# Expert loop with the hidden units on partitions, biases outside the products, and sums made in the output tensor

## The reference, cut to what matters

```python
gate = xt @ Wg + bg
scores, idx = jax.lax.top_k(gate, 2)
h = gelu(einsum('td,edh->eth', xt, W1) + b1[:, None, :])       # 8 experts, 768 -> 384
y = einsum('eth,ehd->etd', h, W2) + b2[:, None, :]             # 384 -> 768
out = einsum('te,etd->td', comb, y)                            # comb: the scores, 0 elsewhere
x = x + out
```

## Time and profile before

| | us |
|---|---|
| median of 3 runs | 1122.59 |
| the profiled execution | 1124.31 |
| its span, first to last instruction | 1122.6 |
| first matmul of the expert loop | 901 |
| last scaled tile | 1102.1 |
| copy to the output issued | 1108.2 |

### The profile page before, as it was taken

The page is one execution under the profiler, slowest core; times in us unless marked ns, Lnnn a source line. Parts: engine busy times, 40 slices in busy tenths (PEclk is TensorE's granted clock), DMA queues, the critical chain, the costliest instruction groups (busy, mean ns, idle before and its releaser), DMA issues.

```text
span 1122.6 us, 17243 instructions
## 1 busy us (share of the span) xinstructions
PE 977.9 (87%) x6460; PEld 708.2 (63%) x6460; DVE 760.7 (68%) x1704; ACT 332.5 (30%) x402; POOL 117.2 (10%) x123
## 2 busy tenths in 40 slices
PE   3799999999789979989988988969887399999991
PEld 2677776765454445545678988858865366666660
DVE  6576788877875686986587898599979823332221
ACT  3561122112004332522333333215335232222220
POOL 3000000000001000000000000000631123333321
PEclk9789999999989999999989999969898599999996
DMA  7350121134341826637687100006056545556546
GB/s 237 105 167 29 57 86 58 57 128 176 107 178 35 297 87 233 185 101 251 225 318 298 47 1 1 1 0 254 5 186 227 209 103 102 109 112 113 110 59 166
DMA packets 58521, 146.44 MB, mean 130 GB/s; under 512 B 11386, under 2 KB 30732, under 8 KB 55434
## 3 DMA queue, kind: packets, MB, share of 16 engines
q1 hardware_dynamic: 49514, 116.25, 29.6%
q0 software_dynamic: 6048, 21.24, 10.0%
q10 hardware_dynamic: 2880, 7.87, 1.8%
HBM read 95.94 MB, written 53.23 MB: 133 GB/s over the span
## 4 chain that ended last, share of the span: by engine, by line
PE 66%; DVE 21%; issue 4%; DMA 4%; ACT 3%; SPq 1%; DVEq 0%; POOLq 0%; ACTq 0%
PE PS L1733 39%; PE PS L1982 12%; DVE arena L1449 3%; PE PS L1809 3%; DVE arena L1455 3%; DVE arena L1493 3%; PE PS L2133 2%; PE PS L1789 1%; PE PS L1820 1%; PE PS L1824 1%; DVE arena L1465 1%; DMA arena<-in_L_gnn_W_dram 1%; DVE arena L1355 1%; DVE arena L1205 1%; DMA arena<-as_d 1%
## 5 line engine op out<-in xcount | busy, mean ns | idle before, releaser
L1733 PE MATMUL PS<-arena 128*128 128x384 f16 (+7 forms) x3396 | 573.0, 322 | 4.6 <-DVE arena L1719 1.9
L1733 PEld LDWEIGHTS PS<-arena 128*128 128x128 f16 (+2 forms) x3396 | 321.0, 99 | 214.8 <-issue 12.2
L1982 PE MATMUL PS<-arena 128*128 128x193 f32 (+1 forms) x1200 | 191.3, 323 | 21.7 <-DVE arena L1455 16.3
L1982 PEld LDWEIGHTS PS<-arena 128*128 128x128 f32 x1200 | 186.7, 200 | 26.3 <-DVE arena L1455 16.0
L1020 ACT ACTIVATE arena<-arena,AS 128x1280 f32<-128x1280 f32 x60 | 81.8, 1363 | 134.0 <-DVE arena L1449 133.8
L1723 DVE TENSOR_SCALAR arena<-PS,arena 128x768 f32<-128x768 f32 x27 | 27.5, 1018 | 138.1 <-PE PS L2159 138.1
L1449 DVE SCALAR_TENSOR_TENSOR arena<-arena,AS 128x1280 f32<-128x1280 f32 x60 | 94.4, 1576 | 0.0
L1455 DVE SCALAR_TENSOR_TENSOR arena<-arena 128x1280 f32<-128x1280 f32 x60 | 90.8, 1513 | 2.5 <-PE PS L1982 2.4
L1257 DVE TENSOR_SCALAR arena<-arena 128x240 f16<-128x240 f16 x324 | 90.0, 278 | 0.0
L1256 DVE TENSOR_SCALAR arena<-arena 128x128 f16<-128x128 f16 x324 | 81.1, 250 | 0.1
L1087 ACT ACTIVATE arena<-PS 128x1536 f16<-128x1536 f16 x27 | 39.2, 1451 | 100.3 <-PE PS L2133 100.3
(11 more groups left out here) (274 smaller groups left out, 953.1 us busy)
## 6 DMA issues: line engine op xcount, KB each, us to landing
arena<-in_L_ffn_W_dram SPq DMA_DIRECT2D x48, 384.0 KB, 4.1
fr_d<-arena SPq DMA_DIRECT2D x48, 384.0 KB, 3.3
arena<-fr_d SPq DMA_DIRECT2D x16, 1152.0 KB, 14.4
arena<-in_x_dram SPq DMA_DIRECT2D x18, 384.0 KB, 5.7
arena<-rr_d SPq DMA_DIRECT2D x4, 1280.0 KB, 8.3
acc_d<-arena SPq DMA_DIRECT2D x11, 384.0 KB, 2.6
g_d<-arena SPq DMA_DIRECT2D x10, 388.0 KB, 2.3
acc_d<-arena ACTq DMA_DIRECT2D x10, 384.0 KB, 2.3
```

Source lines behind the costliest of these rows:

```text
L1733: m = T.matmul(out, left[i][x], right[i][y], start=first and i + r == 0, stop=last and 3 * i + r == n - 1)
L1982: m = T.matmul(ps[b][:, r * (C + 1):(r + 1) * (C + 1)], PT[i % deep][:, d * P:(d + 1) * P], feats, start=t == 0 and r == 0, stop=t == NT - ...
```

## The change

- **Sums in the output.** `sum_out` writes `x` to `out` (98 rows of the last tile in place of 128), `sums_add` adds onto `out` with `bounds_check=N - 1`, which drops the empty slots. The final copy from `acc_d` and its wait go, and so does one blanking DMA of `acc_d`'s spare rows.
- **`up` turned round.** The weights of the expert are now the stationary side and the rows of `XRTP` the moving one, so the 384 hidden units come out on partitions, in HC = 3 groups of 128. `up` is 3 products of 18 matmuls of 128 columns. `turn`, its 3 transposes and `s_ht_psum` go.
- **First bias.** The bias matmul of `up` goes. Three small matmuls before the loop bring the biases of all tiles into PSUM, DVE scales them into `b1t`, and ACT's Gelu takes one column of it as its bias, in 3 activations of 128 columns per tile in place of one of 384.
- **Second bias.** The two bias matmuls of `down` go. GpSimd gathers the 128 rows of `fb2` by expert (`b2_gather`, a third indirect DMA per tile, behind `sums_add`) into `B2`. DVE adds it (a scalar_tensor_tensor of 768) and then multiplies by the score (a tensor_scalar of 768).
- **DVE's order.** `split(i+1)` stands ahead of the scaling of tile i. It reads `Hb` from SBUF, not PSUM.
- `fb3` holds 384 columns, not 1152; three DMAs of `fb2` into `fbs` go.

```diff
-            sp.dma_start(out, acc_d[0:N, :]).then_inc(s_out_done, 16)
-            sp.wait_ge(s_out_done, 16)
...
+            def b2_gather(i):
+                g.indirect_dma_start(out=B2[:, i % 2, :], out_offset=None, in_=fb2,
+                                     in_offset=bass.IndirectOffsetOnAxis(ap=eint[:, i:i + 1].bitcast(U32), axis=0)).then_inc(b2rows_in[i % 2], 16)
...
-                g.indirect_dma_start(out=acc_d, out_offset=bass.IndirectOffsetOnAxis(ap=found[:, i:i + 1].bitcast(U32), axis=0),
-                                     in_=Yb[:, i % 2, :], in_offset=None, compute_op=ALU.add).then_inc(sums_out[i % 2], 16)
+                g.indirect_dma_start(out=out, out_offset=bass.IndirectOffsetOnAxis(ap=found[:, i:i + 1].bitcast(U32), axis=0),
+                                     in_=Yb[:, i % 2, :], in_offset=None, compute_op=ALU.add, bounds_check=N - 1, oob_is_err=False).then_inc(sums_out[i % 2], 16)
             for i in range(3):
                 rows_gather(i)
+            pool.wait_ge(s_slots_ready, 1)
+            pool.wait_ge(s_map_psum, 2)
+            for i in range(2):
+                b2_gather(i)
...
+            def hidden(i):
+                act.wait_ge(s_h_psum, i + 1)
+                if i:
+                    act.wait_ge(s_ht_ready, i)
+                else:
+                    act.wait_ge(s_slots_ready, 2)
+                for c in range(HC):
+                    h = a.activation(Hb[:, c * P:(c + 1) * P], ps[2 + i % 2][:, c * P:(c + 1) * P], ACT.Gelu, bias=b1t[:, c, i:i + 1], scale=1 / UP)
+                h.then_inc(s_h_ready, 1)
...
-                link(V.tensor_copy(ht[:, 0], ps[4][:, 0:HID]))
-                V.tensor_tensor(ht[:, 1], ps[4][:, 0:HID], ht[:, 0], ALU.subtract).then_inc(s_ht_ready, 1)
+                link(V.tensor_copy(ht[:, 0], Hb))
+                V.tensor_tensor(ht[:, 1], Hb, ht[:, 0], ALU.subtract).then_inc(s_ht_ready, 1)
+            split(0)
+            for i in range(NTL):
+                if i + 1 < NTL:
+                    split(i + 1)
+                yb = Yb[:, i % 2, :]
+                dve.wait_ge(b2rows_in[i % 2], 16 * (i // 2 + 1))
                 dve.wait_ge(s_y_psum, i + 1)
                 if i >= 2:
                     dve.wait_ge(sums_out[i % 2], 16 * (i // 2))
-                V.tensor_scalar(Yb[:, i % 2, :].rearrange("p (a n) -> p a n", a=2), PS[:, 5 * 512:7 * 512].rearrange("p (a n) -> p a n", a=2)[:, :, 0:HALF], score[:, 1, i:i + 1], None, ALU.mult).then_inc(s_y_ready, 1)
+                link(V.scalar_tensor_tensor(yb.rearrange("p (a n) -> p a n", a=2), Y, 1 / UP, B2[:, i % 2, :].rearrange("p (a n) -> p a n", a=2), ALU.mult, ALU.add))
+                V.tensor_scalar(yb, yb, score[:, 1, i:i + 1], None, ALU.mult).then_inc(s_y_ready, 1)
...
-                product(ps[2 + i % 2][:, 0:HID], [(XRTP[:, i % 2, 0, k, :], XRTP[:, i % 2, 1, k, :]) for k in range(KC)],
-                        [[FR[:, 0, bass.ds(e, 1), r, k * HID:(k + 1) * HID] for r in (HI, LO)] for k in range(KC)], last=False)
-                T.matmul(ps[2 + i % 2][:, 0:HID], sel[:, i:i + 1].to_broadcast([FBR, P]), fb3[:, 0:HID], start=False, stop=True).then_inc(s_h_psum, 1)
+                for c in range(HC):
+                    m = product(ps[2 + i % 2][:, c * P:(c + 1) * P], [[FR[:, 0, bass.ds(e, 1), r, k * HID + c * P:k * HID + (c + 1) * P] for r in (HI, LO)] for k in range(KC)],
+                                [(XRTP[:, i % 2, 0, k, :], XRTP[:, i % 2, 1, k, :]) for k in range(KC)])
+                m.then_inc(s_h_psum, 1)
...
             for k in range(NS):
                 m = T.matmul(ps[7][:, 0:NQ * NTL].rearrange("p (q i) -> p q i", q=NQ), ohslotb[:, k, :], maps[:, :, k, :], start=k == 0, stop=k == NS - 1)
+            pe.wait_ge(s_slots_ready, 1)
+            pe.wait_ge(s_bias_high, 5)
+            for c in range(HC):
+                m = T.matmul(ps[7][:, (NQ + c) * NTL:(NQ + c + 1) * NTL], fb3[:, c * P:(c + 1) * P], sel[:, 0:NTL], start=True, stop=True, skip_group_check=True)
             m.then_inc(s_map_psum, 1)
```

More of the change, by code:

```diff
@@ L279, in gps_layer @@
         score = v3(small(2 * NTL), 2)
+        b1t = v3(small(HC * NTL), HC)
         seq = small(P)
@@ L287, in gps_layer @@
         FBR = 104
-        fb3 = small((HID + D) // 2, FBR).bitcast(BF16)
+        fb3 = small(HID // 2, FBR).bitcast(BF16)
         sel = small(NTL // 2 + 1, FBR).bitcast(BF16)
-        fbs = reg(O_PT2, HID + D, FBR)
+        fbs = reg(O_PT2, HID, FBR)
         xf_d = nc.dram_tensor("xf_d", (NP + P, D), F32, kind="Internal").ap()
-        acc_d = nc.dram_tensor("acc_d", (NP + P, D), F32, kind="Internal").ap()
+        acc_d = nc.dram_tensor("acc_d", (NP, D), F32, kind="Internal").ap()
         bias_d = nc.dram_tensor("bias_d", (D,), F32, kind="Internal").ap()
@@ L502, in gps_layer @@
         s_y_ready = sem("y_ready")
-        s_out_done = sem("out_done")
         DENSE = 6 * NT
@@ L869, in _ @@
                     sums_add(i - 2)
+                    if i < NTL:
+                        b2_gather(i)
         @block.scalar
@@ L1051, in sum_out @@
                 act.wait_ge(s_x2_ready, t + 1)
-                a.dma_start(acc_d[t * P:(t + 1) * P, :], X[:, t, :]).then_inc(s_x2_out, 16)
+                r = LAST if t == NT - 1 else P
+                a.dma_start(out[t * P:t * P + r, :], X[0:r, t, :]).then_inc(s_x2_out, 16)
             def row_high(t):
@@ L1088, in _ @@
                 if i:
[L1089 to L1095, removed]
+                    hidden(i - 1)
+            hidden(NTL - 1)
         @block.vector
@@ L1710, in _, with split @@
             link(V.tensor_tensor(score[:, 0, :], score[:, 0, :], mapped(2), ALU.add))
-            link(V.tensor_scalar(score[:, 1, :], score[:, 0, :], 128 / UP, None, ALU.mult))
-            for i in range(NTL):
-                dve.wait_ge(s_ht_psum, i + 1)
+            V.tensor_scalar(score[:, 1, :], score[:, 0, :], 128.0, None, ALU.mult)
+            V.tensor_scalar(b1t, ps[7][:, NQ * NTL:(NQ + HC) * NTL].rearrange("p (c i) -> p c i", c=HC), 1 / UP, None, ALU.mult).then_inc(s_slots_ready, 1)
+            dve.wait_ge(s_slots_ready, 2)
+            def split(i):
+                dve.wait_ge(s_h_ready, i + 1)
                 if i >= 2:
@@ L2156, in down @@
                 for c in range(2):
-                    product(ps[5 + c][:, 0:HALF], [(HT[:, i % 2, 0, k, :], HT[:, i % 2, 1, k, :]) for k in range(HC)],
-                            [[FR[:, 1, bass.ds(e, 1), r, k * D + c * HALF:k * D + (c + 1) * HALF] for r in (HI, LO)] for k in range(HC)], last=False)
-                    m = T.matmul(ps[5 + c][:, 0:HALF], sel[:, i:i + 1].to_broadcast([FBR, P]), fb3[:, HID + c * HALF:HID + (c + 1) * HALF], start=False, stop=True)
+                    m = product(ps[5 + c][:, 0:HALF], [(HT[:, i % 2, 0, k, :], HT[:, i % 2, 1, k, :]) for k in range(HC)],
+                            [[FR[:, 1, bass.ds(e, 1), r, k * D + c * HALF:k * D + (c + 1) * HALF] for r in (HI, LO)] for k in range(HC)])
                 m.then_inc(s_y_psum, 1)
@@ L2175, in _ @@
                     rows_in(i + 1)
-                if i:
-                    turn(i - 1)
                 up(i, e)
@@ L2181, in _ @@
                 before = e
-            turn(NTL - 1)
             down(NTL - 1, before)
```

25 lines of the change are left out of this document (9 added, 16 removed).

## The result

The changed kernel takes 1117.13 us, the median of 10 runs (1110.39 to 1118.7). The kernel before took 1124.67 us beside it (1120.92 to 1134.35). The ratio is 0.9919, with a 95% interval of 0.9891 to 0.9947: it is 0.8% faster. The forecast was 1133.5 us, slower by 1.0%, with a range from 1113 to 1148. The time lies in the range, but on the other side of no change. The profiled execution took 1114.72 us with a span of 1113.0, 9.6 us less than the span of before.

The account below looks back on a forecast made before the run. It took TensorE's sequencer to become the bound, 8.29 us a tile against 7.35: 24.5 periods +23, loop start +0.9, tail about +1, copy -14.0, so +10.9 us and 1133.5 us; range 1113 to 1148.

Parts of the forecast that it names:

- What bounds the kernel, and what would be next: Expert loop: the array bounds now at 7.35 us a tile; next is TensorE's sequencer, 0.13 us per address instruction.
- Rival A: Expert loop: addresses shared or hidden, so the array stays the bound at 6.62 us a period; 1091 us, chance 0.11.
- C: Rival in `up`: weight loads don't hide, `up` 5.4 us and the array's sum 9.0; about 1151 us, chance 0.05.
- D: Rival in the loop: sums onto `out` or behind `b2_gather` take over 8.3 us; about 1150 us, chance 0.03.
- The sequencer's work per tile: TensorE's sequencer per tile: 48 addresses 6.24, number load 1.29, waits 0.33, `rows_in` 0.43; sum 8.29 us, the new period.
- the long one: Loading the expert's number each tile: the load takes 0.94 us, not 0.31; 1.29 us up to the next wait.
- the 0.43 for `rows_in`: Sequencer, each tile: handing over the 12 pairs of `rows_in` at 0.036 us each costs 0.43 us.
- break-even: Expert loop: the period at which the change neither gains nor loses, 8.29 - 10.9/25 = 7.85 us.
- The bounds: Sequencer's period: 7.2 us at the low end (0.124 per address, short load), 9.2 at the high end (0.145 per address).
- The bias table: Before the loop: the removed bias columns of `fb3` and its DMAs lie beside other work and are worth nothing.
- The end: After the last scaling: the 14.0 us copy goes, last sums take 6.07 us and the final wait 0.4.
- The tail: Last tile: `down` takes 3.2 us, with a 1.75 us scaling before and after it; the tail adds about 1 us.

Follow-up runs that it names:

- the kernel with the fixed weights: The changed kernel, but `up` reads expert 0's weights at fixed addresses in all tiles, leaving 12 address instructions per tile; 1092.27 us, ratio 0.9721.
- the old `up`: The changed kernel with `up`, its bias matmul and 3 transposes as before the change; 1101.9 us (ratio 0.9812), and 1103.32 us with more rounds.
- the kernels with few loads: The changed kernel with experts' numbers loaded for nine tiles at once: 1116.87 us; also with `up` and `down` groups interleaved on TensorE: 1100.78 us.

## Why the prediction was wrong

*What bounds the kernel, and what would be next.* Right. The address instructions are 48 a tile and 0.124 to 0.13 apart, the sequencer sets the period and the array starves in `up`; without the addresses the period is the array's 6.61, forecast 6.62. Rival A is out by the count of 1296, C by the kernel with the fixed weights, D because in the loop nobody on TensorE waits for sums or gathers, and the sums land in 5.6 us (5.7 before). DVE, ACT and GpSimd stayed under 60%, and the clock at 1.00 in the loop.

*The sequencer's work per tile.* This is the step that failed, in two of its terms. "I take the long one, which all tiles but the first three show" put 1.29 us on the load; it is 0.85 in after and 0.59 in the best kernels (0.30 + 0.286). And the 0.43 for `rows_in` came from 20 pairs handed over in 0.7 us. After's sequencer goes from the wait in front of `rows_in` to the next in 0.165 us, the wait's own 0.11 included, so 12 pairs cost 0.06. The 20 pairs were more than the 17 that the sequencer may be ahead, so their time was probably the array's. Both numbers came from places where the sequencer had time in hand, and there an instruction's distance is no price. The two made the forecast of the period 0.81 us too long; the addresses took 0.11 more than forecast, which leaves 0.70. Over 24.5 periods that is 17 us. The break-even that the text gave, 7.85, was right by its own logic: 7.61 lies under it. With this term right the sum would have given 1116.5 us. That this is so near the 1117.13 is partly luck, since the start of the loop on one side and the end and the tail on the other were off by several us each.

*The bounds.* The lower one, 7.2, took the short load and 0.3 for `rows_in`. The truth lay nearer to it than to the value chosen. A forecast of "slower" at 0.72 leant on two terms that were each read at their dearest.

*The bias table.* The columns that go "lie at 835 to 845 us beside other work and are worth nothing", the text said. Wrong by 3 to 5 us. The row that would have shown a part of it stands in rows 6: line 1624 with a mean of 826 ns. Nine of its ten are 0.66 and one is 2.26. I read this row as a price for a pass with two scalars, and did not ask why its mean lay above the 557 of line 1280.

*The end.* The copy's 14.0 was about right (13.4). The terms "sums 6.07" and "end 0.4" were together short by 2.8 us. The adds onto `out` do not "move the same 128 rows of 3 KB" in the last tile, and land in 3.5 us. But GpSimd's drain replaces the copy as what ends last, and it is longer in the kernels with the gathers.

*The tail.* In the profiled run the last `down` took 4.79 us (the chain of the end, in the section on the result) and not 3.1, as in the second profile. The granted clock was 0.5 from 1097.6 to 1101.0, after 1.95 us in which TensorE waited for the scaling. That cost 1.7 us in this run; in the second profile of the same kernel it fell only from 1102.0 on, after the last matmul.

Together, for the profiled run: forecast +10.9, less 17 for the period, less 8.4 at the start, plus 2.8 for the drain, 1.7 for the clock and a rest of 0.4, is -9.6.

## What to carry to other kernels

The cost of a sequencer instruction must be read where the engine's queue is empty. A duration or distance taken where the sequencer is ahead is how long it was allowed to take. Ask of every mean what its largest member is, and what another engine did at that moment. And where two streams share a sequencer with a limited lead, put the work that needs many addresses between work that needs few: with 3 loads and that order, the turned `up` gives 1100.8 us, as fast as the old `up` (1101.9 and 1103.3) and 1.3% under the changed kernel beside it (1115.1).

## What the runs showed of the hardware

- An address instruction holds TensorE's sequencer for 0.124 us, though its row shows 46 ns, with a longer interval at about every eighth.
- The sequencer ran at most 17 pairs of weight load and matmul ahead of the array, in before, after and the kernels with few loads.
- A load of one value into a register took 0.30 to 1.17 us, one of nine values 0.87 to 2.5.
- GpSimd's DRAIN at the end lasts past the last landing. It took 6.26 us with 54 indirect DMAs in the program and the sums in the output, 7.8 and 8.0 with 54 and the sums in `acc_d`, and 8.48 with 81.
- GpSimd's subtraction on 8 partitions held a DVE pass on 128 partitions for 1.6 us. A pass that reads PSUM was not held beside one on 40.
